# Two edits to a gated cross-attention kernel: where the guards stand in SyncE's queue, and 35 pieces of 46 scores in a top-32 selection

## The reference

```python
Q = (x_text @ Wq).reshape(Bb, Tt, H, DH)            # 4 heads of 32
K = (x_vision @ Wk).reshape(Bb, Gg, H, DH)
scores = jnp.einsum('bthd,bghd->bhtg', Q, K) / np.sqrt(DH).astype(np.float32)
topv, topi = jax.lax.top_k(scores, K_TOP)           # K_TOP = 32
probs = jax.nn.softmax(topv, axis=-1)
attn = jnp.zeros_like(scores).at[bi, hi, ti, topi].set(probs)
attn_mean = attn.mean(axis=1)
c_t = jnp.einsum('btg,bgd->btd', attn_mean, x_vision @ Wv)
```

```python
scores = jnp.einsum('bqhd,bkhd->bhqk', q, k) * scale
weights = jax.nn.softmax(scores, axis=-1)
out = jnp.einsum('bhqk,bkhd->bqhd', weights, v).reshape(B, Lq, D)
```

## Time and profile before

| | us |
|---|---|
| median of 3 runs | 3328.2 |
| lowest, highest | 3325.5, 3335.1 |
| the profiled execution | 3325.9 |
| its span in the profile | 3324.4 |
| busy: PE, DVE, ACT, POOL | 2556.5, 2380.3, 2055.0, 1246.9 |
| first attention | about 200 to 1420 |
| second attention | about 1820 to 3095 |

### The profile page before, as it was taken

How to read it: one execution, slowest core, us unless ns; L and a number is a source line. 1 busy time by engine, 2 the same in 40 slices (tenths; PEclk the granted TensorE clock), 3 DMA queues, 4 the chain that set the end, 5 groups by cost and what they waited for, 6 DMA issues and landing times. The chain is left out here.

```text
span 3324.4 us, 68050 instructions
## 1 busy us (share of the span) xinstructions
PE 2556.5 (77%) x19550; PEld 1303.9 (39%) x19550; DVE 2380.3 (72%) x7659; ACT 2055.0 (62%) x3368; POOL 1246.9 (38%) x1587
## 2 busy tenths in 40 slices
PE   1058888888678888758784589898989889999468
PEld 0035555555445555535321133333333333333335
DVE  5948887787887878636545988888888878883312
ACT  1148888888668888615221077777777777779112
POOL 2037766777557767613102032221111112100332
PEclk9978988898888888889787589999999999999679
DMA  2010010001001001083001633232322323220221
GB/s 54 0 31 32 32 42 33 31 31 50 30 18 46 31 31 42 26 274 95 1 18 29 102 97 89 86 90 81 84 82 84 85 87 85 81 53 2 71 77 45
DMA packets 136744, 195.94 MB, mean 59 GB/s; under 512 B 51842, under 2 KB 104511, under 8 KB 136363
## 3 DMA queue, kind: packets, MB, share of 16 engines
q1 hardware_dynamic: 126350, 152.17, 16.8%
q0 software_dynamic: 10016, 39.46, 3.3%
HBM read 125.38 MB, written 66.62 MB: 58 GB/s over the span
## 5 line engine op out<-in xcount | busy, mean ns | idle before, releaser
L2030 ACT ACTIVATE pb<-sps 128x512 f32<-128x512 f32 (+1 forms) x1664 | 896.6, 596 | 377.3 <-PE sps L1974 363.1
L2056 DVE TENSOR_REDUCE mx<-wps 128x2 f32<-128x802 f32 x1024 | 957.4, 988 | 157.0 <-PE wps L1949 140.7
L986 DVE MAX8 cand<-sc 128x8 f32<-128x51 f32 (+1 forms) x4096 | 562.9, 197 | 193.8 <-issue 162.0
L1987 PE MATMUL ops<-pb,va 128*32 128x256 f32 x6656 | 555.8, 407 | 7.6 <-ACT ot L2036 7.2
L749 PE MATMUL scores<-ctxT,qT 97*128 97x512 f32 (+1 forms) x1024 | 437.6, 576 | 43.8 <-ACT sc L870 42.7
L1949 PE MATMUL wps<-ks,qs 56*128 56x401 bf16 x2048 | 384.7, 361 | 105.1 <-DVE mx L2056 53.2
L1974 PE MATMUL sps<-qs,ks 59*128 59x256 bf16 (+1 forms) x3328 | 363.5, 284 | 70.3 <-DMA qs<-guards 69.8
L1834 POOL COPY va<-vn 128x128 f32<-128x128 f32 (+1 forms) x208 | 49.9, 292 | 796.6 <-PE ops L1987 720.0
L749 PEld LDWEIGHTS scores<-ctxT,qT 97*128 97x128 f32 x1024 | 210.5, 215 | 274.9 <-issue 220.6
L1974 PEld LDWEIGHTS sps<-qs,ks 59*128 59x128 bf16 (+1 forms) x3328 | 120.7, 96 | 411.0 <-ACT pb L2030 242.2
L617 POOL TENSOR_TENSOR prf<-sc,prf 128x1601 f32<-128x1601 f32 x64 | 230.0, 3594 | 119.0 <-ACT prf L877 118.1
(11 more groups left out here) (408 smaller groups left out, 3697.1 us busy)
## 6 DMA issues: line engine op xcount, KB each, us to landing
ks<-keys SPq DMA_DIRECT2D x896, 50.0 KB
keys<-kpb POOLq DMA_DIRECT2D x42, 400.2 KB, 3.3
toep<-kernpad SPq DMA_DIRECT2D x8, 2048.0 KB, 15.0
qs<-queries SPq DMA_DIRECT2D x896, 8.0 KB
values<-vs SPq DMA_DIRECT2D x16, 832.0 KB, 3.7
vn<-values SPq DMA_DIRECT2D x16, 832.0 KB, 4.7
keysf<-kf SPq DMA_DIRECT2D x16, 800.5 KB, 4.6
kfb<-keysf POOLq DMA_DIRECT2D x14, 800.5 KB, 5.5
```

Of the source, the lines that this page charges most:

```text
L986: st.add(v.max(cand[s % 2][:, n, :], sc[s % 4][:, c:c + w]))
L1987: ins = t.matmul(ops[VW * i:VW * i + VW, 0:S], va[par][0:kn(kt), kt, 4 * g + i, :], pb[(UNITS * g + 2 * kt + i % 2) % 8][0:kn(kt), i // 2, :],
L2030: nc.scalar.activation(pb[(UNITS * g + u) % 8][0:rows_, :, :], sps[(UNITS * g + u) % SB][0:rows_, :, :], ACT.Exp).then_inc(p_ready, 1)
L2056: v.tensor_reduce(mx4[:, q, h:h + 2, c], both, AX.X, ALU.max).then_inc(work_read, 1)
```

## The change

```diff
@@ -34,7 +34,7 @@
 GONE = -3e38
 GT = 4
 NG = T // GT
-PICK = 51
+PICK = 46
 PIECES = [(c, min(PICK, NK - c)) for c in range(0, NK, PICK)]
 CHUNKS = [(c, min(512, NK - c)) for c in range(0, NK, 512)]
 
@@ -1915,11 +1915,12 @@
 
             def batch(b, par):
 
-                for g in range(HG - 1):
+                for g in range(HG - 2):
                     load(b + 2, par, g, True)
                 load_values(b + 2, True)
                 guard(b + 1, 1 - par, not (isinstance(b, int) and b == 0))
-                load(b + 2, par, HG - 1, True)
+                for g in range(HG - 2, HG):
+                    load(b + 2, par, g, True)
 
             batch(0, 0)
             with sp.Fori(0, (B - 4) // 2) as i:
```

## The result

| | median us | lowest to highest | runs |
|---|---|---|---|
| before | 3331.7 | 3325.5 to 3337.0 | 4 |
| changed | 3230.0 | 3228.1 to 3231.9 | 4 |

The ratio is 0.9695, 95% interval 0.9674 to 0.9717: 3% faster, 102 us. The prediction was 3190 with a range of 3174 to 3223. The direction was right, but the time is 40 us above the forecast (102 us of gain where 138 were forecast) and outside the range. The profiled execution took 3228.1 us, its span 3226.6.

The account below looks back on a forecast made before the run. It took ACT and PE to bound the first attention and PE's guards waits with the slow clock the second: 3325.9 - 106 - 33 + 1 = 3188, stated as 3190 us, range 3174 to 3223 at about 83%.

Parts of the forecast that it names:

- What bounds the phases: First attention: a ring of ACT and PE, DVE beside it with slack; second: PE waiting for the guards, 69.8 us.
- The uT copies and ACT's list: First attention: uT copies 71.7 us apart throughout, and ACT's waits of note all on PE, none on DVE.
- the batch of 67.8 us: Second attention: each batch falls from 75.5 to 67.8 us, with bounds of 67.2 and about 69.
- The chain of the guards: Second attention boundary: store after 0.24 us, loads after 1.41, PE after 2.22; guards land 3.1 us before PE runs dry.
- So the 14 waits go: Second attention: PE's 14 waits for the guards vanish, 69.8 - 4.5 = 65.3 us.
- the slow clock: Second attention: PE's reduced clock behind each wait also goes, about 3 us a batch; with the waits 106 us.
- What is moved costs nothing: Second attention: the third and fourth groups' later loads stay covered, the third by 12 us; nobody waits.
- Pieces of 46: First attention: 45 us more DVE work, 0.35 us a step, off the path; cost about 1 us at the ends.
- the 33 us that were forecast: First attention: no tile needs select_all with pieces of 46, so two long batches shrink, saving 33.0 us.
- The Trainium skill's rule on small tiles: First attention: each small tile pays some 150 cycles, making three more pieces 60 us; the prediction used the trace's 0.117 us.
- The Trainium skill's rule on the ramp's cost: Clock ramp costs under 1% of a span, at most 33 us in the kernel; the prediction went by the batches' pace.
- rival 1: Second attention: clock stays low behind the boundary from PE's short pauses; only 65.3 us go, 3229 us; chance 8%.

Follow-up runs that it names:

- the second experiment: Pieces of 46 alone, with the loads in the old order, against the kernel before: 3296.2 us, ratio 0.9898 (0.9867 to 0.9928).

## Why the prediction was wrong, point by point

- **What bounds the phases**: right in both. The uT copies and ACT's list held, and so did the batch of 67.8 us, measured as 68.0 wherever no loop turns.
- **The chain of the guards**: right. 0.24 and 1.41 us were taken from the last boundary; the profile after has 0.2 and 1.43, and a landing time of 1.4 us for all 16 stores.
- **"So the 14 waits go", 65.3 us, and with them the slow clock, 106 us in all: this is the step that failed.** It held at nine boundaries. At the five turns of the loop, PE's jump back came to light: 3.6 to 4.3 us without a matmul, and the clock fell to the half level as before. These batches are 75.2 to 76.5 us, 75.7 on average, where 68.0 were to be had: 5 x 7.7 = 38.6 us of the 40 by which the time missed. I had taken the chain that released PE last for the only thing that PE waited for. The row's releaser is what ends last, and what ended a little earlier has no row there. The jump itself was in the trace of the kernel before, had I looked, under the line of the loop:

```profile
L1797 PEldq COMPARE_BRANCH  x6: 83/5870/6167, 2127.7 to 2885.5; - x6
```

These are five branches of 5.5 to 6.2 us and the last, which falls through. Each of the five ends 0.1 to 1.0 us before the guards' last packet lands. So at the turns the guards were not the only thing that held PE, and to take them away could not bring its idle time to nothing. The alternation was there too: at the turns the waits were 5.1 to 6.6 us, between them 3.8 to 4.7, and the boundary that I laid out was one of the second kind. The last boundary, from which I took the new chain, is outside the loop.

- **What is moved costs nothing**: right. PE waits for no `qs<-queries` in the loop, and SP keeps its place.
- **Pieces of 46**: 45 us of DVE's work were forecast. DVE's busy time rose by 7.6 us, from 2380.3 to 2387.9, while two `select_all` of 18.8 us each left it: 45 us. None of it shows on the path. `select_all` gave the 33 us that were forecast, within the interval of the second experiment (24 to 44).
- **The Trainium skill's rule on small tiles** ("VectorE: DVE Perf Modes", section on the TRN2 errata) was rightly left to the trace: 0.113 us a piece with its columns. **The Trainium skill's rule on the ramp's cost** ("TensorE: Matmul & The Clock Gate", Part 1) is not borne out: the low clock behind a standstill costs some 3 us here (75.5 - 68.0 - 4.7 = 2.8 at a boundary of the kernel before, 7.7 - 4.0 = 3.7 at the turns of the changed kernel), so 14 of them in the kernel before were 39 us or 1.2% of its span.
- **The rivals**: the time lies at what rival 1 gave (3229), for another reason. Its mechanism, a clock that stays low by itself, is refuted at the boundaries by the nine that PE passes at the full clock. Elsewhere it was seen twice: at 2069 and 2212 us, behind a pause of 1.15 us for DVE, eight matmuls take 1.08 us, and the two batches concerned are about 1 us longer than the other three of their kind. I had the size of such an outcome and no place for it.

## What to carry to other kernels

When a wait is to be removed at the border of a loop's body, ask what every engine does while it waits: the turn of the loop itself can need time, and the list of waits names only what ended last. Look up the branch under the line of the loop, and list the waits one by one over several turns; where they alternate with the period of the body, the turn is in them. A fallback path that depends on the data should be counted from the inputs before a tile size is chosen: 5 columns decided over 33 us here. The number of pieces cost nothing that could be measured up to 35, and 53 us at 45.

## What was not expected of the hardware

- A jump back of PE's loop in the second attention costs 2.9 to 4.3 us without a matmul and, with the clock that falls behind it, 5.6 to 8.5 us a turn: 2.9 and 3.1 us with four batches in the body, 3.6 to 4.3 with two. In the first attention it costs 0.22 us. DVE and ACT stood idle for about 2 us at theirs. Where only those two were left, the clock still fell at three of the five turns (0.83 over the 10 us there).
- The same batch takes 68.01 us in a loop's body and 66.57 us written out for ACT and DVE. A row of ten maxima in a looped batch takes 9.38 us, and in a written-out one fifteen take 14.10. From first to last start that is 0.932 and 0.936 us each, so the reductions themselves are no slower; the time lies in the gaps, of which the looped group has two more (0.15 and 0.16 us). In the trace a looped batch has 68 register instructions (ALU_OP) on DVE and 153 on ACT, a written-out one none, and DVE is idle for 5.1 us of the one and 4.1 us of the other. That these instructions make the gaps was not tried.

```profile
2037.98 9.38 DVE L2057 TENSOR_REDUCE mx<-wps 128x2 f32<-128x802 f32 x10 [0.15 <-PE wps L1950]
2047.52 4.65 DVE L2057 TENSOR_REDUCE mx<-wps 128x2 f32<-128x802 f32 x5 [0.16 <-PE wps L1950]
...
2040.01 14.10 DVE L2062 TENSOR_REDUCE mx<-wps 128x2 f32<-128x802 f32 x15 [0.34 <-PE wps L1955]
```

The first two rows are the changed kernel's, the third that of the kernel with three loops written out.
